# Twelve decoder blocks in two planned lanes: which lane goes first where, and two units of the last layer cut anew

## The reference, cut to what matters

```
x = x + L0_attn(norm(x));   x = x + L0_xattn(norm(x), ctx);  x = x + L0_ffn(norm(x))
x = x + L1_attn(norm(x));   x = x + L1_xattn(ctx, norm(x));  x = x + L1_ffn(norm(x))
x = x + L2_attn(norm(x));   x = x + L2_xattn(norm(x), ctx);  x = x + L2_ffn(norm(x))
x = x + L3_attn(norm(x));   x = x + L3_xattn(norm(x), ctx);  x = x + L3_ffn(norm(x))
```

```
dt = softplus(dt_r @ W + b);  h = exp(dt*A) * h + dt*B*x;  y = sum_n h*C          # L3_attn
a1 = softmax(q1 k1 * s);  a2 = softmax(q2 k2 * s);  out = (a1 - lam*a2) @ v        # L3_xattn
```

## Time and profile before

| | us |
|---|---|
| median of three runs | 2274.02 |
| the profiled execution itself | 2271.46 |
| its span, first to last instruction | 2269.7 |
| busy: PE 1858.6 (82%), DVE 1619.4 (71%), ACT 1009.9 (44%), POOL 626.4 (28%) | |

### The profile page before, as it was taken

The page is one execution under the profiler, slowest core; times in us unless marked ns, Lnnn a source line. Parts: engine busy times, 40 slices in busy tenths (PEclk is TensorE's granted clock), DMA queues, the critical chain, the costliest instruction groups (busy, mean ns, idle before and its releaser), DMA issues. The chain is left out here.

```text
span 2269.7 us, 31071 instructions
## 1 busy us (share of the span) xinstructions
PE 1858.6 (82%) x11250; PEld 1064.2 (47%) x11250; DVE 1619.4 (71%) x3582; ACT 1009.9 (44%) x1680; POOL 626.4 (28%) x564
## 2 busy tenths in 40 slices
PE   4778888879888989999998777778876686689974
PEld 2445554637363333477776556555522232243431
DVE  5666858676768879743637887884489979984656
ACT  1225545464643462743334444442364364326552
POOL 0002414242332020100003555530156627631000
...
DMA packets 19223, 44.18 MB, mean 19 GB/s; under 512 B 5323, under 2 KB 7935, under 8 KB 18047
## 3 DMA queue, kind: packets, MB, share of 16 engines
...
## 5 line engine op out<-in xcount | busy, mean ns | idle before, releaser
L2397 PE MATMUL lane_banks<-l_attn_lane_hc,base 128*128 128x512 f32 x256 | 167.4, 768 | 85.5 <-DVE l_attn_lane_hc L2539 85.2
L2481 POOL TENSOR_TENSOR l_attn_lane_u<-l_attn_lane_xp,l_attn_lane_bn 128x512 f32<-128x512 f32 x128 | 188.3, 1501 | 123.7 <-ACT l_attn_lane_bn L2452 110.0
L605 POOL TENSOR_SCALAR lane_next_rstd<-lane_next_mv 128x4 f32<-128x4 f32 x48 | 11.9, 249 | 672.5 <-DVE lane_next_mv L582 672.5
L2530 DVE TENSOR_TENSOR_SCAN l_attn_lane_h<-l_attn_lane_da,l_attn_lane_u 128x512 f32<-128x512 f32 x128 | 191.7, 1542 | 1.4 <-PE lane_banks L2399 1.0
L1732 ACT ACTIVATE l_ffn_lane_hT<-lane_banks,weights 128x512 f32<-128x512 f32 x128 | 87.9, 687 | 141.6 <-PE lane_banks L1686 141.0
L1778 DVE SCALAR_TENSOR_TENSOR l_ffn_lane_eo<-lane_banks,l_ffn_lane_sel,l_ffn_lane_eo 128x128 f32<-128x128 f32 x224 | 63.0, 344 | 105.2 <-PE lane_banks L1708 104.7
L2397 PEld LDWEIGHTS lane_banks<-l_attn_lane_hc,base 128*128 128x128 f32 x256 | 57.6, 241 | 159.1 <-DVE l_attn_lane_hc L2539 123.5
L1530 ACT ACTIVATE l_attn_lane_ex<-lane_banks 128x512 f32<-128x512 f32 x160 | 84.1, 668 | 98.0 <-PE lane_banks L1444 97.3
L1708 PEld LDWEIGHTS lane_banks<-weights,l_ffn_lane_hT 128*128 128x128 f32 x1024 | 119.8, 192 | 16.1 <-issue 12.4
L1708 PE MATMUL lane_banks<-weights,l_ffn_lane_hT 128*128 128x128 f32 x1024 | 122.8, 276 | 0.9 <-DVE l_ffn_lane_eo L1778 0.9
L2058 POOL TENSOR_TENSOR l_attn_lane_qb<-l_attn_lane_qT,base 128x512 f32<-128x512 f32 x64 | 88.9, 1402 | 63.4 <-PE lane_banks L1946 52.2
...
## 6 DMA issues: line engine op xcount, KB each, us to landing
...
```

Of the source, the lines that this page charges most:

```text
L2397: pe.matmul(ps(2 + c), w("ident"), hc[:, c, :], start=(n == 1), stop=(n == NS)).then_inc(*s.up("state_added"))
L2481: g.tensor_tensor(u[:, i % 3, :], dtx[:, c, :], bn[:, n % 2, :], ALU.mult).then_inc(*s.up("u_ready"))
L2530: v.tensor_tensor_scan(h[:, c, :], da[:, i % 3, :], u[:, i % 3, :], 0.0, ALU.mult, ALU.add).then_inc(*s.up("scanned"))
```

## The change

The planner's chosen kinds become `l0_attn`, `l1_attn` and `l3_xattn` in place of `l2_attn`. In `l3_attn` the first bf16 part is cast by ACT and the f32 copy of the PSUM bank goes, and for the second channel block (c = 1) the two instructions of `d` and the one of `dtx` go from DVE to POOL. `l3_xattn` takes its heads four at a time: `keyed` puts four matmuls into all four banks, one for each row group, two exponentials take them, `apply` goes to banks 0 and 1 and `heads` to 2 and 3, so that the next four heads begin when DVE has read the last. The instructions of exponentials, copies, turns and divisions are the same in size and number. Shown is the core of it; left out are the parts of `apply`, `heads` and `copy_out` that only name other banks.

```diff
--- before.py
+++ after.py
@@ -2429,6 +2429,7 @@
         yield
         act.wait_ge(*s.at("dbc_in_psum", 1))
         act.activation(dbc[:, :], ps(1)[0:R, :], ACT.Copy).then_inc(*s.up("dbc_ready"))
+        act.activation(part[:, :], ps(2)[0:96, :], ACT.Copy).then_inc(*s.up("first_part"))
         yield
         act.wait_ge(*s.at("dt_in_psum", C))
         for c in range(C):
@@ -2469,13 +2470,22 @@
         norm.wait(g)
         ln.pool_steps.link(g.tensor_tensor(x, x, bc(w("a3_bout"), NT), ALU.add))
         g.tensor_tensor(x, x, norm.xn[:, :, :], ALU.add).then_inc(*s.up("residual_added"))
+
+        yield
+        g.wait_ge(*s.at("e_ready", 2))
+        ln.pool_steps.link(g.tensor_scalar(d[:, 1, :], e[:, 1, :], 1.0, -1.0, ALU.add, ALU.add))
+        g.tensor_tensor(d[:, 1, :], e[:, 1, :], d[:, 1, :], ALU.subtract).then_inc(*s.up("lost_ready"))
         for n in range(NS):
             for c in range(C):
                 i = C * n + c
+                if i == 1:
+                    yield
+                    g.wait_ge(*s.at("dt_ready", 2))
+                    ln.pool_steps.link(g.tensor_tensor(dtx[:, 1, :], dt[:, 1, :], xs[:, 1, :], ALU.mult))
                 yield
                 g.wait_ge(*s.at("bn_ready", n + 1))
-                if n == 0:
-                    g.wait_ge(*s.at("dtx_ready", c + 1))
+                if i == 0:
+                    g.wait_ge(*s.at("dtx_ready", 1))
                 if i >= 3:
                     g.wait_ge(*s.at("scanned", i - 2))
                 g.tensor_tensor(u[:, i % 3, :], dtx[:, c, :], bn[:, n % 2, :], ALU.mult).then_inc(*s.up("u_ready"))
@@ -2495,30 +2505,31 @@
                                    op0=ALU.add, op1=ALU.mult).then_inc(*s.up("xs_ready"))
 
         yield
-        v.wait_ge(*s.at("dbc_in_psum", 1))
-        st.step(v.tensor_copy(bc3, ps(2)[0:96, :]))
-        st.link(v.tensor_copy(part[:, :], ps(2)[0:96, :]))
-        st.link(v.scalar_tensor_tensor(out=bc3, in0=part[:, :], scalar=w("a3_parts", 0, 1)[0:96, :], in1=bc3, op0=ALU.mult, op1=ALU.add))
+        v.wait_ge(*s.at("first_part", 1))
+        st.link(v.scalar_tensor_tensor(out=bc3, in0=part[:, :], scalar=w("a3_parts", 0, 1)[0:96, :], in1=ps(2)[0:96, :],
+                                       op0=ALU.mult, op1=ALU.add))
         st.link(v.tensor_copy(part[:, :], bc3))
         v.scalar_tensor_tensor(out=parts[:, :], in0=part[:, :], scalar=w("a3_parts", 1, 2)[0:96, :], in1=bc3,
                                op0=ALU.mult, op1=ALU.add).then_inc(*s.up("parts_ready"))
 
+        yield
+        v.wait_ge(*s.at("e_ready", 1))
+        st.link(v.tensor_scalar(d[:, 0, :], e[:, 0, :], 1.0, -1.0, ALU.add, ALU.add))
+        st.link(v.tensor_tensor(d[:, 0, :], e[:, 0, :], d[:, 0, :], ALU.subtract))
         for c in range(C):
             yield
-            v.wait_ge(*s.at("e_ready", c + 1))
-            st.link(v.tensor_scalar(d[:, c, :], e[:, c, :], 1.0, -1.0, ALU.add, ALU.add))
-            st.link(v.tensor_tensor(d[:, c, :], e[:, c, :], d[:, c, :], ALU.subtract))
-        for c in range(C):
-            yield
             v.wait_ge(*s.at("ln_ready", c + 1))
+            if c == 1:
+                v.wait_ge(*s.at("lost_ready", 1))
             st.link(v.tensor_tensor(logs[:, c, :], logs[:, c, :], d[:, c, :], ALU.add))
             yield
             v.wait_ge(*s.at("z_ready", c + 1))
             v.scalar_tensor_tensor(out=dt[:, c, :], in0=z[:, c, :], scalar=0.0, in1=logs[:, c, :], op0=ALU.max, op1=ALU.add)\
              .then_inc(*s.up("dt_ready"))
-            yield
-            v.wait_ge(*s.at("dt_ready", c + 1))
-            v.tensor_tensor(dtx[:, c, :], dt[:, c, :], xs[:, c, :], ALU.mult).then_inc(*s.up("dtx_ready"))
+            if c == 0:
+                yield
+                v.wait_ge(*s.at("dt_ready", 1))
+                v.tensor_tensor(dtx[:, 0, :], dt[:, 0, :], xs[:, 0, :], ALU.mult).then_inc(*s.up("dtx_ready"))
         for n in range(NS):
             for c in range(C):
                 i = C * n + c
@@ -2565,7 +2576,7 @@
     vt = sb("vt", [S2, D])
     va = sb("va", [S2, 2, H, 32])
     mp = sb("mp", [P, NT, 2, R, 32])
-    ex = sb("ex", [S2, 4, 2, T])
+    ex = sb("ex", [S2, 2, R, T])
     oS = sb("oS", [P, 2, T])
     rden = sb("rden", [P, NT * R])
     parts = sb("parts", [P, NT, R, 8])
...
-        def keyed(g):
-
-            i, e, a, _ = fill(g // 2)
-            yield
-            if g == 0:
+        def keyed(k, half):
+
+            i, a = k // 2, k % 2
+            yield
+            if k == 0 and half == 0:
                 pe.wait_ge(*s.at("maxima_ready", 2))
+            elif half == 0:
+                pe.wait_ge(*s.at("oS_ready", 2 * k))
+                pe.wait_ge(*s.at("cat_ready", 2 * k))
             else:
-                pe.wait_ge(*s.at("exp_done", g))
-            for b in range(2):
-                last = pe.matmul(ps(b)[0:S2, :], km[group[2 * e + b], i, 2 * a + g % 2, :], ops[group[2 * e + b], i, :], start=True, stop=True)
+                pe.wait_ge(*s.at("exp_done", 4 * k + 2))
+            for r in range(R):
+                last = pe.matmul(ps(r)[0:S2, :], km[group[r], i, 2 * a + half, :], ops[group[r], i, :], start=True, stop=True)
             last.then_inc(*s.up("keyed_in_psum"))
 
...
-        for n in range(FILLS + 1):
-            if n < FILLS:
-                yield from keyed(2 * n)
-            if n >= 1:
-                yield from apply(n - 1)
-            if n < FILLS:
-                yield from keyed(2 * n + 1)
-            if n >= 1:
-                yield from heads(n - 1)
...
-        for g in range(2 * FILLS):
-            yield
-            act.wait_ge(*s.at("keyed_in_psum", g + 1))
-            if g >= 4 and g % 2 == 0:
-                act.wait_ge(*s.at("applied", g // 2 - 1))
-            act.activation(ex[:, g % 4, :, :], banks(0, 2)[0:S2, :, :], ACT.Exp, scale=scale).then_inc(*s.up("exp_done"))
-            if g % 2 == 0 and g >= 2:
-                yield from copy_out(g // 2 - 1)
...
+        for k in range(FILLS // 2):
+            for half in range(2):
+                for e in range(2):
+                    yield
+                    act.wait_ge(*s.at("keyed_in_psum", 2 * k + half + 1))
+                    act.activation(ex[:, half, 2 * e:2 * e + 2, :], banks(2 * e, 2)[0:S2, :, :], ACT.Exp, scale=scale).then_inc(*s.up("exp_done"))
+            for e in range(2):
+                yield from copy_out(2 * k + e)
...
-    order = plan(streams, {ln.done: (ln.index, [u[1] is l2_attn for u in units]) for ln, units in zip(net.lanes, plans)})
+    order = plan(streams, {ln.done: (ln.index, [u[1] in (l0_attn, l1_attn, l3_xattn) for u in units]) for ln, units in zip(net.lanes, plans)})
```

More of the change, by code:

```diff
@@ L2579, in fill @@
     def fill(n):
-        i, e, a = n // 4, n // 2 % 2, n % 2
-        return i, e, a, 8 * i + 4 * e + a
+        i, a, e = n // 4, n // 2 % 2, n % 2
+        return i, a, e, 8 * i + 4 * e + a
     def tensor(pe):
@@ L2644, in heads @@
             pe.wait_ge(*s.at("oS_ready", n + 1))
-            if n >= 1:
-                pe.wait_ge(*s.at("cat_ready", n))
             for t in range(NT):
-                last = pe.transpose(ps(2)[:, tile(t)], oS[:, n % 2, tile(t)], w("ident"))
+                last = pe.transpose(ps(2 + n % 2)[:, tile(t)], oS[:, n % 2, tile(t)], w("ident"))
             last.then_inc(*s.up("heads_in_psum"))
-        for n in range(FILLS + 1):
-            if n < FILLS:
-                yield from keyed(2 * n)
-            if n >= 1:
-                yield from apply(n - 1)
-            if n < FILLS:
-                yield from keyed(2 * n + 1)
-            if n >= 1:
-                yield from heads(n - 1)
-        yield from norm.tensor(pe, ps(3), norm.to_come)
+        for k in range(FILLS // 2):
+            yield from keyed(k, 0)
+            yield from keyed(k, 1)
+            for e in range(2):
+                yield from apply(k, e)
+            for e in range(2):
+                if e == 0:
+                    yield
+                    pe.wait_ge(*s.at("exp_done", 4 * k + 4))
+                yield from heads(2 * k + e)
+        yield
+        pe.wait_ge(*s.at("cat_ready", FILLS - 1))
+        yield from norm.tensor(pe, ps(2), norm.to_come)
         yield
@@ L2687, in copy_out @@
                 act.wait_ge(*s.at("heads_in_psum", n - 1))
-            act.activation(oS[:, n % 2, :], ps(3), ACT.Copy).then_inc(*s.up("oS_ready"))
-        for g in range(2 * FILLS):
-            yield
-            act.wait_ge(*s.at("keyed_in_psum", g + 1))
-            if g >= 4 and g % 2 == 0:
-                act.wait_ge(*s.at("applied", g // 2 - 1))
-            act.activation(ex[:, g % 4, :, :], banks(0, 2)[0:S2, :, :], ACT.Exp, scale=scale).then_inc(*s.up("exp_done"))
-            if g % 2 == 0 and g >= 2:
-                yield from copy_out(g // 2 - 1)
-        yield from copy_out(FILLS - 1)
-        yield from norm.scalar(act, ps(3), norm.to_come)
```

(12 more changed lines are left out.)

10 lines of the change are left out of this document (4 added, 6 removed).

## The result

The changed kernel takes 2284.0 us (median of 20 runs, 2270.8 to 2290.1), the kernel before, on the same chip, 2272.7 (2266.8 to 2275.5). The ratio is 1.0044, with a 95% interval from 1.0032 to 1.0056: slower by 11 us, where 2212 was forecast and 2262 was the upper end. The profiled execution has a span of 2278.1 us (before 2269.7). The 20 executions differ by more than those of the kernel before, and the clock goes with it: the shortest span, 2269.0 us, had a mean granted clock of 0.867, the longest, 2288.3, one of 0.857.

The account below looks back on a forecast made before the run. No engine was taken to bound the whole, leaving mainly waits to win. Terms -5 -10 -6 -15 -24 = -60 gave 2211 us on the profiled execution and 2214 on the median; the forecast was 2212, range 2172 to 2262.

Parts of the forecast that it names:

- `l0_attn` -5: In `l0_attn`, two score reads go before lane 1's search in the first pass, halving one wait: -5 us, bounds +2 and -10.
- `l1_attn` -10: In `l1_attn`, one lane's maxima stand among the other's second phase: -10 us, between -32 (DVE bounds) and +68 (slow clock).
- The slower rival: In `l1_attn`, PE's second-phase work is granted only 1.2 GHz: +68 in place of -10, 2290 us; chance 0.10.
- `l2_attn` 0: `l2_attn` loses its rule, but lane 0's lead there stays about the same: 0 us, bounds 8 either way.
- `l2` cross and `l2_ffn` -6: In `l2` cross attention and `l2_ffn`, more of lane 0's part lies beside lane 1's `l2_attn`: -6 us, bounds -20 and +5.
- `l3_attn` -15: In `l3_attn`, four parts (instructions, dead stretch, fewer colliding scans, scans beside set-ups), -8 -7 -13 +13: -15 us, bounds -30 and +10.
- The first part: In `l3_attn`, DVE loses copy, cast and three instructions moved to POOL in each unit: -8 us, within 2.6 to 12.6 gained.
- The dead stretch: In `l3_attn`, 1830 to 1854: both lanes no longer set up at once, which gives back 7 of 24 us.
- Third and fourth: In `l3_attn`: fewer steps with colliding scans, -13 us; the same steps standing beside set-ups and `l3_xattn`, +13.
- `l3_xattn` and the end -24: Two `l3_xattn` units shorten by 13 us (lane 1's second some 76), the `l3_ffn` end by 11: -24, bounds 0 and -36.
- the clock falls: Rival in `l1_attn`: PE's second-phase work, spread among the first's, is granted 1.2 GHz: 2290 us, chance 0.10.
- the order does nothing: Rival for the whole kernel: only the edits work, -8 in `l3_attn` and -13 in `l3_xattn`: 2250 us, chance 0.12.

Follow-up runs that it names:

- e2: The changed kernel with the old kind, `l2_attn`, in the planner's rule, so both `l3` edits alone: 2263.9 us, ratio 0.9965.
- e8: The changed kernel (both edits) with `l0_attn` and `l2_attn` as the rule's kinds: 2262.9 us, ratio 0.9964.
- e14: The changed kernel (both edits) with `l0_attn` alone in the rule: 2276.7 us, ratio 1.0024.
- e5: The changed kernel without `l3_xattn` in the rule (kinds `l0_attn` and `l1_attn`): 2279.7 us, ratio 1.0033.
- e13: The changed kernel (both edits) with `l0_attn`, `l1_attn` and `l2_attn` in the rule: 2287.1 us, ratio 1.0069.
- e4: The kernel before with the `l3_xattn` edit alone: 2263.8 us, ratio 0.9960.
- e12: The kernel before with `l0_attn` and `l1_attn` in the rule in place of `l2_attn`, without the edits: 2285.5 us, ratio 1.0066.
- e15: The changed kernel with the first turn in `l3_xattn` given to lane 1 and not lane 0: 2281.8 us, ratio 1.0046.
- e11: The changed kernel with scores and `keyed` matmuls of `l3_xattn` made twice in lane 1's second unit: 2288.4 us, ratio 1.0075.

## Why the prediction was wrong

The runs split the change along one path, medians: before 2272, both edits -8 (e2), `l0_attn`'s turn -1 (e8), `l2_attn`'s turn gone +14 (e14), `l1_attn`'s +3 (e5), `l3_xattn`'s +4 (the changed kernel). The steps, in my order:

- *`l0_attn` -5.* The lanes' mean gains 4.2 us at its end, but lane 1, which sets the end, is 2.5 later there and 1.7 earlier at the end of `l0_ffn`. As a term: -1, too small to be told from nothing.
- *`l1_attn` -10.* The clock did rise (0.80 for 0.75), and the mean of the lanes' ends gains 3.9. But DVE was to be used better, and it is busy for 80% of the stage, for 83% before. The gain is lane 0's (-25, to 223.9 us) and the cost lane 1's (+17, to 261.5, where 234 was forecast), and `l1_ffn`, full of PE work (239.7 of 241), gives back 2.7 of the 17. The failed step is to count the gain of two lanes as one of the program. The slower rival saw that the clock can fall under PE records that look full, but in the wrong place: it fell in `l3_xattn`, not here.
- *`l2_attn` 0.* A miss of 14, past its own bound of 8: I said the lead there was about what it was, so the turn did nothing. The failed step is to call it 0: it is worth 14 us (e14 for e8), 12 of them there at the end of `l2_attn`. A lead brought from `l1_attn` replaces part of it (lane 1: 276 us with the turn, 283 with the lead, 297 with neither), and with that lead there the turn itself costs 7 (e13 for e5). By which wait stays open.
- *`l2` cross and `l2_ffn` -6.* Lane 1 -9.5: right.
- *`l3_attn` -15.* The first part was right as DVE's time and wrong as the program's: DVE's instructions sum to 8.6 us less (e2 for e4), and lane 1's units got 2 us longer. POOL's `tensor_scalar` takes 2.45 us, its subtraction 1.27, its `dtx` 1.28; I had used 1.08. The whole term's bounds were added up too small: by its own four parts they are -33 and +13, not -30 and +10. The dead stretch did not go: 1825 to 1835 has DVE at 5.8 of 10 us. Third and fourth, in the changed kernel:

```profile
L2541 DVE TENSOR_TENSOR_SCAN l_attn_lane_h<-l_attn_lane_da,l_attn_lane_u 128x512 f32<-128x512 f32 x128 | 188.3, 1508 | 18.4 <-ACT l_attn_lane_da L2461 13.5 <-issue 3.1 <-POOL l_attn_lane_u L2491 1.1
L2550 DVE TENSOR_TENSOR l_attn_lane_hc<-l_attn_lane_h,lane_banks 128x512 f32<-128x512 f32 x128 | 80.1, 671 | 8.8 <-PE lane_banks L2399 8.6
```

  The groups (busy, mean ns, idle before) lie between 1590 and 2060. Colliding scans fell from 55 to 50 of 128, scan time by 4.4 and not 13; and DVE now idles 27 us ahead of its scans and products, where before it had 1.5. Half of that idle time ends with ACT's `da`, where I had let DVE alone lead: I had put +13 for a lane that scans beside a set-up. The maxima of lane 0 do stand ahead of lane 1's scans, in pairs with 0.79 us of waiting ahead of each:

```profile
1998.78 1.51 DVE L2747 TENSOR_REDUCE l_xattn_lane_mp<-lane_banks 128x8 f32<-128x616 f32 x2 [0.79 <-PE lane_banks L2618]
2001.08 1.51 DVE L2747 TENSOR_REDUCE l_xattn_lane_mp<-lane_banks 128x8 f32<-128x616 f32 x2 [0.79 <-PE lane_banks L2618]
```

  That was named as what would make it wrong. Lane 1's last `l3_attn` unit takes 197.5 us, as in the kernel before, and 186.5 in e5, where that turn is away: the turn eats what that unit would gain. The +10.2 of the stage lie in lane 1's first unit (201.5 us for 191.3). It is 202.7 in e12, which has the old `l3_attn`, and 194.7 in e2, which has the old order, so they come mostly from the order.
- *`l3_xattn` and the end -24.* From lane 1's last `l3_attn` instruction it is 216 us, for 228 before and 204 forecast. `keyed` is 1.10 (1.2 forecast), and the -11 in `l3_ffn` came (-13.4). What failed is the lone unit of 76 us; alone it took 95.6. The sum took the clock of the stretch in which both lanes were there, and it put ScalarE's table loads at nothing, though lane 0's `l3_ffn` beside it takes another function. (Its round of 10.3 also counts one `apply` and one `heads` where a round has two of each, 1.98 and 1.14 us together at a clock of 1.00, so that the 78.6 of e15 come near the 76 partly by luck.) The loads, with the gates between them, held its exponentials back by 8.2 us. An estimate for the clock, from the round shown: two `keyed` 4.0 us for 2.2, two `apply` 3.64 for 1.98, two `heads` 2.2 for 1.1, 4.5 us in a round at half clock; two of the four rounds ran at it nearly throughout and two in part, which makes some 13. The two together are a little more than the 16 to 20 us by which the unit is too long, since not all of it lies on the chain. The Trainium skill's page "TensorE: Matmul & The Clock Gate" (section "HAM oscillation — how this bites in real kernels") describes such a fall to the slow clock where TensorE waits for DMA between short bursts of matmuls; the trace agrees as to the fall (0.63 in that stretch), with waits for ScalarE and VectorE in place of DMA. I had weighed the clock for `l1_attn` alone.

  Over the kernels with the new `l3_xattn` both causes grow together, so these runs can't part them:

| lane 1's last unit | table loads | mean clock | us |
|---|---|---|---|
| e2, e8 | 1 | 0.91 | 79.6 |
| e5 | 7 | 0.81 | 89.5 |
| the changed kernel | 13 | 0.77 | 95.6 |
| e11 (PE work added) | 13 | 0.85 | 99.8 |

Of the rivals, "the clock falls" (2290) came nearest in number, by luck: the clock did not fall in `l1_attn`, and not by 78 us; "the order does nothing" (2250) was too good: the order costs 20 us beside edits worth 8. What stays open: why each half of the `l3_attn` edit costs alone, by which wait `l2_attn`'s turn is worth its 14 us, and how the lone unit's 16 to 20 us divide between the slow clock and the table loads. An order that keeps lane 0's gates together, so that the loads go and the clock stays, was not run.
